# Attention with one PSUM bank for the products with V and three for the ring, the block's copy one unit sooner on ScalarE, and transposes ahead of products in a unit

## The chip, the cores and the metric

The kernel runs on one core of a Trainium2 chip. The metric is the time of one execution on the device in microseconds (us).

## What is computed

One block of a MetaFormer on 8 images of 512 channels by 32 x 32 positions (1024 tokens): a layer norm over channels, attention with 8 heads of 64 with its projections and residual, then a layer norm over tokens and a mixture of 16 experts, each of which takes the 128 tokens with the highest affinities of every image.

```python
def reference(x, Wq, bq, Wk, bk, Wv, bv, Wo, bo, gate_weight, w1, b1, w2, b2):
    x = x + attention(ln_c(x))         # 8 heads, softmax over 1024 keys
    t = to_tokens(x)
    t = t + experts(ln_t(t))           # gate, top 128 of each expert, gelu MLP, scatter-add
    return from_tokens(t)
```

The parameter names are shortened here (`L0_conv_Wq` and so on), and `attention` stands for q, k, v projections, softmax(q k / 8) v and the output projection.

## The kernel before

Every engine has its own program, written out by hand in `attention` as a function per engine; the order of the work is the order of the code, and engines meet by semaphores alone. Products run on single-precision operands split into a high part and a low part, so most results in PSUM are read twice: ScalarE writes the high part to SBUF, VectorE subtracts it and writes the low part.

An image's attention is 64 units (`UNITS`): 4 pairs of heads (`PAIRS`), 2 heads each, 8 slices of 128 queries. A unit s means, in this order over three engines:

- TensorE, `scores`: 4 matmuls into one of two places of `S` (L865).
- VectorE, `maximum` (L696); ScalarE, `exponentials` into `prob` (L494).
- TensorE, `turn_probs` (L876): 8 transposes of `prob`, in two sets of four (c = 0, 1), each set into one bank of `ring`.
- ScalarE, `high_of_probs` (L503), and VectorE, the low part (L754): each set from `ring` into `PT`, which holds two blocks.
- TensorE, `product_with_v` (L908): two units make a block m of 256 queries; a block takes 32 matmuls of V and `PT` into one of two banks `O[:, m % 2]`, in four parts of 4 matmuls of each high and low (part 0 and 1 in one unit, 2 and 3 in the next).
- ScalarE, `copy_output` (L552): the block from `O` into `oHL`; GpSimd adds its two halves and scales them.

TensorE in its loop step s does the scores of unit s, the transposes of unit s-2 and two parts of block (s-5)//2 (`turn_and_multiply`). ScalarE in its step s does the exponential of unit s-1, at even s a copy of block (s-8)//2, then `high_of_probs` of unit s-2. For an even unit u that one waits until block u//2-2 is finished, since it shares its half of `PT`:

```python
if u // 2 >= 2 and u % 2 == 0 and c == 0:
    act.wait_ge(pv_done, j * BLOCKS + u // 2 - 1)
```

At s = 16, 32 and 48 `project_pair` (L818) makes q and k of the next pair: 48 matmuls into the ring, 12 for each of 4 results. The step before it does no products; they come first in the step of the projection.

The 8 banks of PSUM are `S` (4), `ring` (2, used in turn by number k of the ring's step) and `O` (2). A step of the ring waits until VectorE has read the step two before it (`ring_lo`); part 0 of block m waits until block m-2 has been copied (`o_copied`). Between images, `O` takes the V projection (two banks in turn), the gate's logits and their transposes, and the ring the norm's transposes.

After all images, `experts` runs; nothing of it is touched.

Of the kernel before, what the change touches and what calls it, by code (L numbers as in the profile page):

```python
# [16 lines left out]
F32 = mybir.dt.float32  # L17
# [6 lines left out]
P = 128  # L24
# [29 lines left out]
def ring_probs(u, c):  # L54

    return NT + 4 * min(PAIRS, (u + 2) // UP + 1) + 2 * u + c

# [29 lines left out]
def attention(nc, x, wT, b_row, b_col, gate, out, n2_dram, aff_dram, ident):  # L87
# [8 lines left out]
    with ExitStack() as ctx:  # L96
# [61 lines left out]
        ring = ctx.enter_context(nc.psum_tensor("ring", [P, 2, 512], F32))  # L158
        O = ctx.enter_context(nc.psum_tensor("O", [P, 2, 512], F32))
# [303 lines left out]
        def _(act):  # L463
# [5 lines left out]
            def high_of_norm(j, i):  # L469
                k = ring_norm(i)  # L470
                act.wait_ge(ring_filled, j * RING + k + 1)
                nc.scalar.activation(nT[:, 0, :, i * P:(i + 1) * P],
                                     ring[:, k % 2, :].rearrange("p (k t) -> p k t", k=KC),
                                     ACT.Copy).then_inc(ring_hi, 1)
# [6 lines left out]
            def high_of_proj(j, p, r0=0, r1=4):  # L481
                for r in range(r0, r1):
                    k = ring_proj(p, r)
                    act.wait_ge(ring_filled, j * RING + k + 1)
                    cols = slice((r % 2) * 512, (r % 2) * 512 + 512)
                    for odd in range(2):
                        rows = slice(D * odd, D * odd + D)
                        dst = kd[rows, odd, 0, cols] if r < 2 else qs[rows, odd, cols]
                        nc.scalar.activation(dst, ring[rows, k % 2, :], ACT.Identity,
                                             bias=bqk[rows, 1 - r // 2, p:p + 1]).then_inc(ring_hi if odd else even_hi, 1)  # L490
# [6 lines left out]
            def high_of_probs(j, u):  # L497
                for c in range(2):
                    k = ring_probs(u, c)
                    act.wait_ge(ring_filled, j * RING + k + 1)  # L500
                    if u // 2 >= 2 and u % 2 == 0 and c == 0:
                        act.wait_ge(pv_done, j * BLOCKS + u // 2 - 1)
                    nc.scalar.activation(PT[:, 0, u // 2 % 2, 4 * c:4 * c + 4, u % 2 * P:u % 2 * P + P],  # L503
                                         ring[:, k % 2, :].rearrange("p (m q) -> p m q", m=4),
                                         ACT.Copy).then_inc(ring_hi, 1)
# [33 lines left out]
            def image(b, last):  # L539
# [5 lines left out]
                def copy_output(m):  # L545
                    act.wait_ge(pv_done, b * BLOCKS + m + 1)
                    if m >= BLOCKS - HEAD_BLOCKS:
                        cols = slice(m % HEAD_BLOCKS * QC, m % HEAD_BLOCKS * QC + QC)
                        nc.scalar.activation(Rs[D:2 * D, cols], O[D:2 * D, m % 2, QC:2 * QC], ACT.Copy)
# [37 lines left out]
                def copy_logits(h):  # L587
                    act.wait_ge(logits, b * 2 + h + 1)
                    nc.scalar.activation(affT[:, 512 * h:512 * h + 512], O[0:E, h, :], ACT.Copy
                                         ).then_inc(logits_copied, 1)  # L590
# [19 lines left out]
                for i in range(2):  # L610
                    act.wait_ge(affT_filled, b * 2 + i + 1)
                    nc.scalar.activation(affT[:, 512 * i:512 * i + 512], O[0:E, 1 - i, :], ACT.Copy
                                         ).then_inc(affT_copied, 1)
# [4 lines left out]
        def _(dve):  # L618
# [41 lines left out]
            def low_of_norm(j, i):  # L660
                k = ring_norm(i)
                dve.wait_ge(ring_hi, j * RING + k + 1)
                nc.vector.tensor_tensor(nT[:, 1, :, i * P:(i + 1) * P],
                                        ring[:, k % 2, :].rearrange("p (k t) -> p k t", k=KC),
                                        nT[:, 0, :, i * P:(i + 1) * P].bitcast(F32),
                                        ALU.subtract).then_inc(ring_lo, 1)

            def sum_of_v(j, i):

                dve.wait_ge(v_filled, j * NT + i + 1)  # L670
                if i >= 4:
                    dve.wait_ge(v_lo, j * NT + i - 3)
                nc.vector.tensor_tensor(tok[:, i % 4, :], O[:, i % 2, :], bv_bc[:, :], ALU.add).then_inc(v_sum, 1)

            def low_of_proj(j, p, beside=None):
                for r in range(4):
                    if beside is not None:
                        beside(r)
                    k = ring_proj(p, r)
                    cols = slice((r % 2) * 512, (r % 2) * 512 + 512)  # L680
                    for odd in range(2):
                        if odd:
                            dve.wait_ge(ring_hi, j * RING + k + 1)
                        else:
                            dve.wait_ge(even_hi, j * (4 * PAIRS) + 4 * p + r + 1)
# [3 lines left out]
                        last_lo = nc.vector.scalar_tensor_tensor(  # L689
                            out=lo, in0=ring[rows, k % 2, :], scalar=bqk[rows, 1 - r // 2, p:p + 1],  # L690
                            in1=hi.bitcast(F32), op0=ALU.add, op1=ALU.subtract)
                    last_lo.then_inc(ring_lo, 1)
# [31 lines left out]
            def image(b, last):  # L724
# [8 lines left out]
                for s in range(2, UNITS + 2):  # L733
# [16 lines left out]
                    for c in range(2):  # L750
# [4 lines left out]
                                                ring[:, k % 2, :].rearrange("p (m q) -> p m q", m=4),  # L755
# [42 lines left out]
                lgp = O[:, 0, 0:NT * E].rearrange("p (i e) -> p i e", e=E)  # L798
# [15 lines left out]
        def _(pe):  # L814
# [8 lines left out]
            def turn_norm(j, i, first):  # L823

                k = ring_norm(i)
                pe.wait_ge(norm_done[0], j * NT + i + 1)
                if not first or i >= 2:
                    pe.wait_ge(ring_lo, j * RING + k - 1)
                for c in range(KC):
                    last_t = nc.tensor.transpose(ring[:, k % 2, c * P:(c + 1) * P], xt[:, i, c * P:(c + 1) * P], ident)  # L830
                last_t.then_inc(ring_filled, 1)

            def project_v(j, i):
# [3 lines left out]
                products(O[:, i % 2, :], [(nT[:, l, c, i * P:(i + 1) * P], wv[:, w, c, :])  # L837
                                          for c in range(KC) for l, w in HL]).then_inc(v_filled, 1)

            def project_pair(j, p, r0=0, r1=4):  # L840
# [29 lines left out]
            def turn_probs(j, u, c):  # L870
# [3 lines left out]
                pe.wait_ge(ring_lo, j * RING + k - 1)  # L874
                for m in range(4):
                    last_t = nc.tensor.transpose(ring[:, k % 2, m * P:(m + 1) * P],  # L876
# [19 lines left out]
            def image(b, last):  # L896
                def product_with_v(m, part):

                    head = m // QB
                    if part == 0:  # L900
                        if m == 0:
                            pe.wait_ge(v_lo, b * NT + NT)
                        if m >= 2:
                            pe.wait_ge(o_copied, b * BLOCKS + m - 1)
                        pe.wait_ge(ring_lo, b * RING + ring_probs(2 * m + 1, 1) + 1)
                    for t in range(2 * part, 2 * part + 2):
                        for l in range(2):
                            last_mm = nc.tensor.matmul(  # L908
                                O[:, m % 2, 0:QC],
# [6 lines left out]
                def inverse_sums(m):  # L916
# [4 lines left out]
                    for j in range(2):  # L921
                        last_t = nc.tensor.transpose(O[:, m % 2, QC + j * P:QC + (j + 1) * P],
# [94 lines left out]
                for i in range(NT):  # L1017
                    pe.wait_ge(n2_copied, b * NT + i + 1)
                    last_mm = products(O[0:E, i // 4, i % 4 * P:i % 4 * P + P],
# [11 lines left out]
                for i in range(NT):  # L1031
                    last_t = nc.tensor.transpose(O[:, 0, i * E:(i + 1) * E], affT[:, i * P:(i + 1) * P],
# [7 lines left out]
                for h in range(2):  # L1040
                    for i in range(4):
                        last_t = nc.tensor.transpose(O[0:E, 1 - h, i * P:(i + 1) * P], aff[:, 4 * h + i, :], ident)
# [392 lines left out]
```

## Time and profile before

| | before |
|---|---|
| median of 3 runs | 3221.65 us (3219.97 to 3221.84) |
| profiled execution | 3216.83 us |
| its span, first to last instruction | 3215.0 us |
| mean granted TensorE clock | 0.984 |
| two units in the steady part of a head | 5.45 us |

In views by groups, a line of the kernel, its engine and operation are followed by busy time, mean duration and the idle time of the engine just before, with what ended it ("<-ACT PT L503": ScalarE's write at L503). In the order of time, a row has the start, the duration until the last of its instructions ended, and how many there are. PE is TensorE, PEld its loading of weights, ACT ScalarE, DVE VectorE, POOL GpSimd.

### The profile page before, as it was taken

The numbers are of one execution on the slowest core, as the hardware profiler recorded it, in microseconds if no ns is written. First come the engines' busy times: TensorE is split into PE (matmuls) and PEld (weight loads), VectorE is DVE, ScalarE is ACT, GpSimd is POOL, SyncE is SP. The second block draws the span as 40 slices with busy tenths as digits, with TensorE's granted clock in tenths as the row PEclk, the third lists the DMA queues.
The fourth block names the chain that finished last, engine by engine and source line by source line (L and its number), as shares of the span: only waits on it lengthen the run. The fifth ranks groups of instructions, "written<-read, shape, count | busy, mean of one in ns | idle before, by whom it ended". The sixth has DMA issues, their size and how long they took to land. (4 is left out here: it accounts for less than half of the span.)

```text
span 3215.0 us, 49747 instructions
## 1 busy us (share of the span) xinstructions
PE 3059.6 (95%) x18114; PEld 2627.4 (82%) x18114; DVE 2278.2 (71%) x3481; ACT 1850.1 (58%) x3353; POOL 1093.1 (34%) x1112
## 2 busy tenths in 40 slices
PE   6999999999999999999999999999917999999998
PEld 5988889888888888887988889888816788888886
DVE  5887688688768877876888688587775655655653
ACT  4876678477657857774876678477612333333332
POOL 1225224322512351252225124322513444444443
PEclk9999999999999999999999999999968999999999
DMA  7122121321321132113123121311224666666564
GB/s 236 37 60 106 64 63 50 112 67 37 105 88 50 50 115 77 37 57 118 58 60 109 61 63 57 105 41 37 63 96 94 135 141 133 135 143 137 129 144 59
DMA packets 121438, 283.59 MB, mean 88 GB/s; under 512 B 22417, under 2 KB 30609, under 8 KB 110481
## 3 DMA queue, kind: packets, MB, share of 16 engines
q1 hardware_dynamic: 92560, 213.72, 20.1%
q0 software_dynamic: 28672, 67.13, 11.8%
q8 instruction: 130, 2.13, 0.3%
q14 instruction: 76, 0.61, 0.1%
HBM read 173.08 MB, written 74.15 MB: 77 GB/s over the span
## 5 line engine op out<-in xcount | busy, mean ns | idle before, releaser
L754 DVE TENSOR_TENSOR PT<-ring,PT 128x512 fp32r<-128x512 f32 x1024 | 676.5, 686 | 160.4 <-ACT PT L503 142.2
L503 ACT ACTIVATE PT<-ring 128x512 fp32r<-128x512 f32 x1024 | 582.7, 597 | 169.8 <-PE ring L876 87.2
L908 PE MATMUL O<-PT,V 128*128 128x256 f32 x4096 | 673.0, 289 | 0.0
L696 DVE TENSOR_REDUCE nmax<-S 128x1 f32<-128x1024 f32 x512 | 619.8, 1211 | 71.7 <-PE S L865 71.7
L876 PE MATMUL ring<-ident,prob 128*128 128x128 f32 x4096 | 614.1, 273 | 15.3 <-DVE PT L754 12.9
L908 PEld LDWEIGHTS O<-PT,V 128*128 128x128 f32 x4096 | 575.4, 189 | 40.2
L865 PE MATMUL S<-kd,qs 128*128 128x512 f32 x2048 | 599.0, 414 | 2.7 <-ACT prob L494 1.7
L494 ACT ACTIVATE prob<-S,nmax 128x1024 f32<-128x1024 f32 x512 | 571.3, 1116 | 36.4 <-DVE nmax L696 36.4
L432 POOL COPY oS<-oHL 64x256 f32<-64x256 f32 x256 | 100.9, 394 | 1282.3 <-ACT oHL L552 1276.3
L876 PEld LDWEIGHTS ring<-ident,prob 128*128 128x128 f32 x4096 | 463.9, 139 | 55.3 <-issue 49.5
L865 PEld LDWEIGHTS S<-kd,qs 128*128 128x128 f32 x2048 | 347.2, 189 | 50.5 <-issue 6.0
L1389 PE MATMUL p<-ws,hT 128*128 128x512 f32 x1536 | 375.6, 397 | 0.7 <-DVE hT L1295 0.7
L1352 PE MATMUL p<-xT,ws 128*128 128x512 f32 x1536 | 355.0, 390 | 1.5 <-DVE xT L1280 1.5
L1352 PEld LDWEIGHTS p<-xT,ws 128*128 128x128 f32 x1536 | 289.4, 188 | 62.0 <-issue 1.9
L1389 PEld LDWEIGHTS p<-ws,hT 128*128 128x128 f32 x1536 | 281.2, 188 | 57.7 <-DVE hT L1295 1.9
L1189 POOL DMA_INDIRECT out_dram<-y,idxc x128 | 202.7, 1584 | 282.5 <-ACT y L1257 250.2
L818 PE MATMUL ring<-nT,wqk 128*128 128x512 f32 x1152 | 267.1, 391 | 3.7 <-DVE PT L754 3.7
L818 PEld LDWEIGHTS ring<-nT,wqk 128*128 128x128 f32 x1152 | 214.4, 188 | 51.0 <-issue 7.9
L1245 ACT ACTIVATE hf<-p,b1s 128x512 f32<-128x512 f32 x128 | 88.3, 690 | 233.0 <-PE p L1352 233.0
L434 POOL TENSOR_TENSOR oT<-oHL,oS 64x256 f32<-64x256 f32 x256 | 188.9, 738 | 20.5
L1232 ACT ACTIVATE xT<-xr 128x512 fp32r<-128x512 f32 x128 | 73.0, 598 | 211.0 <-PE xr L1362 211.0
L947 PE MATMUL S<-wo,nT 128*128 128x512 f32 x768 | 191.3, 398 | 0.0
(115 smaller groups left out, 3457.7 us busy)
## 6 DMA issues: line engine op xcount, KB each, us to landing
kd<-kd SPq DMA_DIRECT2D x128, 256.0 KB, 3.6
wraw<-w_dram SPq DMA_DIRECT2D x32, 1024.0 KB, 7.3
wqk<-wqk_split SPq DMA_DIRECT2D x24, 1024.0 KB, 4.8
xt<-x_dram SPq DMA_DIRECT2D x16, 1024.0 KB, 7.5
Rs<-rinv_rows SPq DMA_DIRECT2D x56, 256.0 KB, 3.4
PT<-wv_split SPq DMA_DIRECT2D x7, 2048.0 KB, 8.9
oT<-x_dram SPq DMA_DIRECT2D x24, 512.0 KB, 3.3
out_dram<-oT SPq DMA_DIRECT2D x48, 256.0 KB, 8.3
```

The costliest lines, as they stand in the source:

```text
L494: nc.scalar.activation(prob[:, s % 2, :], S[:, s % 2, :], ACT.Exp, bias=nmax[:, s:s + 1], accum_out=rsum[:, s:s + 1]).then_inc(exp_done, 1)
L503: nc.scalar.activation(PT[:, 0, u // 2 % 2, 4 * c:4 * c + 4, u % 2 * P:u % 2 * P + P], ring[:, k % 2, :].rearrange("p (m q) -> p m q", m=4 ...
L696: nc.vector.tensor_reduce(nmax[:, s:s + 1], S[:, s % 2, :], AX.X, ALU.max, negate=True).then_inc(max_done, 1)
L754: nc.vector.tensor_tensor(PT[:, 1, here[0], here[1], here[2]], ring[:, k % 2, :].rearrange("p (m q) -> p m q", m=4), PT[:, 0, here[0], her ...
L818: last_mm = nc.tensor.matmul(dst, l, r, start=(n == 0), stop=(n == len(pairs) - 1))
L865: last_mm = nc.tensor.matmul(S[:, s % 2, 512 * m:512 * m + 512], qs[:, odd, i * P:(i + 1) * P], kd[:, odd, l, 512 * m:512 * m + 512], star ...
L876: last_t = nc.tensor.transpose(ring[:, k % 2, m * P:(m + 1) * P], prob[:, u % 2, (4 * c + m) * P:(4 * c + m + 1) * P], ident)
L908: last_mm = nc.tensor.matmul(O[:, m % 2, 0:QC], V[:, t, head // 2, 2 * (head % 2):2 * (head % 2) + 2, :].rearrange("p h d -> p (h d)"), PT ...
L947: last_mm = nc.tensor.matmul(S4[:, i % 4, :], oS[:, l, c, i * P:(i + 1) * P], wo[:, w, c, :], start=(c + n == 0), stop=(c == KC - 1 and n ...
L1189: pool.indirect_dma_start(out=out_rows, out_offset=bass.IndirectOffsetOnAxis(ap=idxc[:, k, G * g + j:G * g + j + 1], axis=0), in_=y[:, g, ...
L1352: last = nc.tensor.matmul(dst, l, r, start=(n == 0), stop=(n == len(pairs) - 1))
L1389: prod = nc.tensor.matmul(p2[:, j, :], hT[:, l, c, j * P:(j + 1) * P], ws[:, k, w, KC + c, :], start=(c + n == 0), stop=(c == KC - 1 and n ...
```

## The change

`O` becomes one bank (`[P, 2 * QC]`), the ring gets three. From the first set of transposes of unit 3 on, each image's ring steps go round three banks, before that round two (`SLOT`, `LAST_USE`); each waits for the step that last used its bank. Everything outside the block loop that used two banks of `O` uses `wide(0)`, the bank `O`, and `wide(1)`, the ring's third. Part 0 of block m waits for the copy of block m-1. ScalarE copies block (s-7)//2 at odd s, and in a unit the transposes of set c come ahead of the products of part c.

```diff
+def ring_slots():
+
+    narrow = ring_probs(3, 0), RING
+    slots, used, last_use = [], {}, []
+    for k in range(2 * RING):
+        i = k % RING
+        slot = (i - narrow[0]) % 3 if narrow[0] <= i < narrow[1] else i % 2
+        slots.append(slot)
+        last_use.append(used.get(slot, k) - RING)
+        used[slot] = k
+    return slots[RING:], last_use[RING:]
+
+
+SLOT, LAST_USE = ring_slots()
...
-        ring = ctx.enter_context(nc.psum_tensor("ring", [P, 2, 512], F32))
-        O = ctx.enter_context(nc.psum_tensor("O", [P, 2, 512], F32))
+        ring = ctx.enter_context(nc.psum_tensor("ring", [P, 3, 512], F32))
+        O = ctx.enter_context(nc.psum_tensor("O", [P, 2 * QC], F32))
+
+        def wide(i):
+
+            return O[:, :] if i == 0 else ring[:, 2, :]
...
-                    nc.scalar.activation(oHL[:, m % 2, :], O[:, m % 2, 0:QC], ACT.Copy).then_inc(o_copied, 1)
+                    nc.scalar.activation(oHL[:, m % 2, :], O[:, 0:QC], ACT.Copy).then_inc(o_copied, 1)
...
-                    if s >= 8 and s % 2 == 0:
-                        copy_output((s - 8) // 2)
+                    if s >= 7 and s % 2 == 1:
+                        copy_output((s - 7) // 2)
                     high_of_probs(b, s - 2)
                     if s in EARLY_AT:
                         high_of_output(EARLY_AT.index(s))
+                copy_output(BLOCKS - 3)
                 high_of_probs(b, UNITS - 1)
                 high_of_output(EARLY)
-                copy_output(BLOCKS - 3)
+                copy_output(BLOCKS - 2)
                 if not last:
                     root(0, b + 1, slice(0, NT))
-                copy_output(BLOCKS - 2)
                 high_of_output(EARLY + 1)
...
                     k = ring_proj(p, r)
-                    pe.wait_ge(ring_lo, j * RING + k - 1)
-                    products(ring[:, k % 2, :],
+                    if j * RING + LAST_USE[k] >= 0:
+                        pe.wait_ge(ring_lo, j * RING + LAST_USE[k] + 1)
+                    products(ring[:, SLOT[k], :],
...
                 pe.wait_ge(exp_done, j * UNITS + u + 1)
-                pe.wait_ge(ring_lo, j * RING + k - 1)
+                if j * RING + LAST_USE[k] >= 0:
+                    pe.wait_ge(ring_lo, j * RING + LAST_USE[k] + 1)
...
-                        if m >= 2:
-                            pe.wait_ge(o_copied, b * BLOCKS + m - 1)
+                        if m >= 1:
+                            pe.wait_ge(o_copied, b * BLOCKS + m)
...
                     for c in range(2):
+                        turn_probs(b, u, c)
                         if m >= 0:
                             product_with_v(m, 2 * half + c)
-                        turn_probs(b, u, c)
```

How it moves ScalarE's work, in the first head of an image, here before. L494 is the exponential, L503 the split of a set of transposes (the one with `pv_done` waits for a block's last product), L552 the copy of a block:

```order
L494 ACTIVATE prob,rsum<-S,nmax 128x1024 [waits max_done,ring_filled]
L503 ACTIVATE PT<-ring 128x4x128 [waits ring_filled] x2
L494 ACTIVATE prob,rsum<-S,nmax 128x1024 [waits max_done,ring_filled]
L552 ACTIVATE oHL<-O 128x256 [waits o_sum,pv_done]
L503 ACTIVATE PT<-ring 128x4x128 [waits pv_done,ring_filled]
L503 ACTIVATE PT<-ring 128x4x128 [waits ring_filled]
L494 ACTIVATE prob,rsum<-S,nmax 128x1024 [waits max_done,ring_filled]
L503 ACTIVATE PT<-ring 128x4x128 [waits ring_filled] x2
```

And after the change, from the same exponential, where the lines are L515, L524 and L573:

```order
L515 ACTIVATE prob,rsum<-S,nmax 128x1024 [waits max_done,ring_filled]
L573 ACTIVATE oHL<-O 128x256 [waits o_sum,pv_done]
L524 ACTIVATE PT<-ring 128x4x128 [waits ring_filled] x2
L515 ACTIVATE prob,rsum<-S,nmax 128x1024 [waits max_done,ring_filled]
L524 ACTIVATE PT<-ring 128x4x128 [waits pv_done,ring_filled]
L524 ACTIVATE PT<-ring 128x4x128 [waits ring_filled]
L515 ACTIVATE prob,rsum<-S,nmax 128x1024 [waits max_done,ring_filled]
L573 ACTIVATE oHL<-O 128x256 [waits o_sum,pv_done]
```

The copy moved from behind the second exponential after a wait for `pv_done` to behind the first; two splits and an exponential stand between that wait and the copy of the block that it waited for.

TensorE's order where one block ends and the next begins, before. L865 are scores, L876 transposes, L908 products with V; the wait for `o_copied` is for block m-2:

```order
L908 MATMUL O<-PT,V 128x256 x4
L876 MATMUL ring<-ident,prob 128x128 [waits ring_lo,exp_done]
L876 MATMUL ring<-ident,prob 128x128 x3
L908 MATMUL O<-PT,V 128x256 x4
L876 MATMUL ring<-ident,prob 128x128 [waits ring_lo,exp_done]
L876 MATMUL ring<-ident,prob 128x128 x3
L865 MATMUL S<-kd,qs 128x512 [waits exp_done]
L865 MATMUL S<-kd,qs 128x512 x3
L908 MATMUL O<-PT,V 128x256 [waits ring_lo,o_copied]
L908 MATMUL O<-PT,V 128x256 x3
```

And after the change (L887, L899, L931), where the wait for `o_copied` is for block m-1:

```order
L931 MATMUL O<-PT,V 128x256 x4
L899 MATMUL ring<-ident,prob 128x128 [waits ring_lo,exp_done]
L899 MATMUL ring<-ident,prob 128x128 x3
L931 MATMUL O<-PT,V 128x256 x4
L887 MATMUL S<-kd,qs 128x512 [waits exp_done]
L887 MATMUL S<-kd,qs 128x512 x3
L899 MATMUL ring<-ident,prob 128x128 [waits ring_lo,exp_done]
L899 MATMUL ring<-ident,prob 128x128 x3
L931 MATMUL O<-PT,V 128x256 [waits ring_lo,o_copied]
L931 MATMUL O<-PT,V 128x256 x3
L899 MATMUL ring<-ident,prob 128x128 [waits ring_lo,exp_done]
L899 MATMUL ring<-ident,prob 128x128 x3
```

The last four products of a block now stand behind the second set of transposes and right ahead of the scores, and between them and the next block's first product there are the scores and one set of transposes.

## Rows read from the trace of the kernel before

**Rows 1.** The page, busy time of each engine with its share of the span.
```profile
PE 3059.6 (95%) x18114; PEld 2627.4 (82%) x18114; DVE 2278.2 (71%) x3481; ACT 1850.1 (58%) x3353; POOL 1093.1 (34%) x1112
```

**Rows 2.** Groups by line: busy us, mean ns of one | idle before.
```profile
L908 PE MATMUL O<-PT,V 128*128 128x256 f32 x4096 | 673.0, 289 | 0.0
...
L503 ACT ACTIVATE PT<-ring 128x512 fp32r<-128x512 f32 x1024 | 582.7, 597 | 169.8 <-PE ring L876 87.2 <-PE O L908 69.7 <-PE O L922 8.8
...
L552 ACT ACTIVATE oHL<-O 128x256 f32<-128x256 f32 x256 | 99.1, 387 | 1.0
```

**Rows 3.** Order of time, TensorE, 434 to 441 us: start, duration, instructions.
```profile
434.48 0.71 PE L908 MATMUL O<-PT,V 128*128 128x256 f32 x4
...
435.39 1.17 PE L865 MATMUL S<-kd,qs 128*128 128x512 f32 x4
...
436.39 0.62 PE L908 MATMUL O<-PT,V 128*128 128x256 f32 x4
...
436.85 0.60 PE L876 MATMUL ring<-ident,prob 128*128 128x128 f32 x4
...
437.21 0.71 PE L908 MATMUL O<-PT,V 128*128 128x256 f32 x4
...
437.76 0.60 PE L876 MATMUL ring<-ident,prob 128*128 128x128 f32 x4
...
440.84 0.47 PE L865 MATMUL S<-kd,qs 128*128 128x512 f32 x1
```

**Rows 4.** Order of time, ScalarE, 434 to 441 us.
```profile
435.29 1.09 ACT L503 ACTIVATE PT<-ring 128x512 fp32r<-128x512 f32 x2 [0.38 <-PE O L908]
...
436.26 1.12 ACT L494 ACTIVATE prob<-S,nmax 128x1024 f32<-128x1024 f32 x1
...
438.89 1.11 ACT L494 ACTIVATE prob<-S,nmax 128x1024 f32<-128x1024 f32 x1
...
439.98 0.39 ACT L552 ACTIVATE oHL<-O 128x256 f32<-128x256 f32 x1
```

**Rows 5.** Order of time around a projection: TensorE, then VectorE, then ScalarE.
```profile
394.98 0.71 PE L908 MATMUL O<-PT,V 128*128 128x256 f32 x4
...
398.24 1.19 PE L908 MATMUL O<-PT,V 128*128 128x256 f32 x8
...
399.59 11.12 PE L818 MATMUL ring<-nT,wqk 128*128 128x512 f32 x48 [0.15 <-DVE PT L754]
...
410.90 1.20 PE L908 MATMUL O<-PT,V 128*128 128x256 f32 x8
...
413.13 0.63 PE L876 MATMUL ring<-ident,prob 128*128 128x128 f32 x4
...
414.52 0.63 PE L908 MATMUL O<-PT,V 128*128 128x256 f32 x4
...
411.47 1.51 DVE L689 SCALAR_TENSOR_TENSOR qs<-ring,bqk,qs 64x512 fp32r<-64x512 f32 x2 [0.49 <-ACT qs L489]
...
413.07 0.69 DVE L754 TENSOR_TENSOR PT<-ring,PT 128x512 fp32r<-128x512 f32 x1
...
413.68 1.21 DVE L696 TENSOR_REDUCE nmax<-S 128x1 f32<-128x1024 f32 x1
...
414.99 1.12 ACT L494 ACTIVATE prob<-S,nmax 128x1024 f32<-128x1024 f32 x1 [0.60 <-DVE nmax L696]
```

**Rows 6.** Order of time, ScalarE, a copy of the output's high part.
```profile
543.65 0.63 ACT L543 ACTIVATE nT<-oT 128x512 fp32r<-128x512 f32 x1
544.17 1.12 ACT L494 ACTIVATE prob<-S,nmax 128x1024 f32<-128x1024 f32 x1
```

**Rows 7.** Stretches: length, busy (count) of PE, PEld, DVE, ACT, POOL; granted clock.
```profile
69.00:76.00 7.00, 4.70 (x19) 3.26 (x19) 4.08 (x5) 4.22 (x7) 0.00 (x0) 0.76 0.57 209
2546.00:2552.00 6.00, 4.42 (x22) 3.33 (x22) 4.39 (x7) 1.21 (x2) 4.78 (x5) 1.00 0.47 131
434.00:441.00 7.00, 7.00 (x56) 6.66 (x55) 6.31 (x9) 5.91 (x13) 1.53 (x4) 1.00 0.01 1
```

More of the change, by code:

```diff
@@ L472, in high_of_norm @@
                 nc.scalar.activation(nT[:, 0, :, i * P:(i + 1) * P],
-                                     ring[:, k % 2, :].rearrange("p (k t) -> p k t", k=KC),
+                                     ring[:, SLOT[k], :].rearrange("p (k t) -> p k t", k=KC),
                                      ACT.Copy).then_inc(ring_hi, 1)
@@ L488, in high_of_proj @@
                         dst = kd[rows, odd, 0, cols] if r < 2 else qs[rows, odd, cols]
-                        nc.scalar.activation(dst, ring[rows, k % 2, :], ACT.Identity,
+                        nc.scalar.activation(dst, ring[rows, SLOT[k], :], ACT.Identity,
                                              bias=bqk[rows, 1 - r // 2, p:p + 1]).then_inc(ring_hi if odd else even_hi, 1)
@@ L503, in high_of_probs @@
                     nc.scalar.activation(PT[:, 0, u // 2 % 2, 4 * c:4 * c + 4, u % 2 * P:u % 2 * P + P],
-                                         ring[:, k % 2, :].rearrange("p (m q) -> p m q", m=4),
+                                         ring[:, SLOT[k], :].rearrange("p (m q) -> p m q", m=4),
                                          ACT.Copy).then_inc(ring_hi, 1)
@@ L663, in low_of_norm @@
                 nc.vector.tensor_tensor(nT[:, 1, :, i * P:(i + 1) * P],
-                                        ring[:, k % 2, :].rearrange("p (k t) -> p k t", k=KC),
+                                        ring[:, SLOT[k], :].rearrange("p (k t) -> p k t", k=KC),
                                         nT[:, 0, :, i * P:(i + 1) * P].bitcast(F32),
@@ L672, in sum_of_v @@
                     dve.wait_ge(v_lo, j * NT + i - 3)
-                nc.vector.tensor_tensor(tok[:, i % 4, :], O[:, i % 2, :], bv_bc[:, :], ALU.add).then_inc(v_sum, 1)
+                nc.vector.tensor_tensor(tok[:, i % 4, :], wide(i % 2), bv_bc[:, :], ALU.add).then_inc(v_sum, 1)
             def low_of_proj(j, p, beside=None):
@@ L689, in low_of_proj @@
                         last_lo = nc.vector.scalar_tensor_tensor(
-                            out=lo, in0=ring[rows, k % 2, :], scalar=bqk[rows, 1 - r // 2, p:p + 1],
+                            out=lo, in0=ring[rows, SLOT[k], :], scalar=bqk[rows, 1 - r // 2, p:p + 1],
                             in1=hi.bitcast(F32), op0=ALU.add, op1=ALU.subtract)
@@ L754, in image @@
                         nc.vector.tensor_tensor(PT[:, 1, here[0], here[1], here[2]],
-                                                ring[:, k % 2, :].rearrange("p (m q) -> p m q", m=4),
+                                                ring[:, SLOT[k], :].rearrange("p (m q) -> p m q", m=4),
                                                 PT[:, 0, here[0], here[1], here[2]].bitcast(F32),
@@ L797, in image @@
                 dve.wait_ge(logits_turned, b + 1)
-                lgp = O[:, 0, 0:NT * E].rearrange("p (i e) -> p i e", e=E)
+                lgp = wide(0)[:, 0:NT * E].rearrange("p (i e) -> p i e", e=E)
                 nc.vector.tensor_reduce(gmax[:, :], lgp, AX.X, ALU.max).then_inc(soft, 1)
@@ L827, in turn_norm @@
                 if not first or i >= 2:
-                    pe.wait_ge(ring_lo, j * RING + k - 1)
+                    pe.wait_ge(ring_lo, j * RING + LAST_USE[k] + 1)
                 for c in range(KC):
-                    last_t = nc.tensor.transpose(ring[:, k % 2, c * P:(c + 1) * P], xt[:, i, c * P:(c + 1) * P], ident)
+                    last_t = nc.tensor.transpose(ring[:, SLOT[k], c * P:(c + 1) * P], xt[:, i, c * P:(c + 1) * P], ident)
                 last_t.then_inc(ring_filled, 1)
@@ L836, in project_v @@
                     pe.wait_ge(v_sum, j * NT + i - 1)
-                products(O[:, i % 2, :], [(nT[:, l, c, i * P:(i + 1) * P], wv[:, w, c, :])
+                products(wide(i % 2), [(nT[:, l, c, i * P:(i + 1) * P], wv[:, w, c, :])
                                           for c in range(KC) for l, w in HL]).then_inc(v_filled, 1)
@@ L873, in turn_probs @@
                 pe.wait_ge(exp_done, j * UNITS + u + 1)
-                pe.wait_ge(ring_lo, j * RING + k - 1)
+                if j * RING + LAST_USE[k] >= 0:
+                    pe.wait_ge(ring_lo, j * RING + LAST_USE[k] + 1)
                 for m in range(4):
-                    last_t = nc.tensor.transpose(ring[:, k % 2, m * P:(m + 1) * P],
+                    last_t = nc.tensor.transpose(ring[:, SLOT[k], m * P:(m + 1) * P],
                                                  prob[:, u % 2, (4 * c + m) * P:(4 * c + m + 1) * P], ident)
@@ L908, in product_with_v @@
                             last_mm = nc.tensor.matmul(
-                                O[:, m % 2, 0:QC],
+                                O[:, 0:QC],
                                 V[:, t, head // 2, 2 * (head % 2):2 * (head % 2) + 2, :].rearrange("p h d -> p (h d)"),
@@ L1018, in image @@
                     pe.wait_ge(n2_copied, b * NT + i + 1)
-                    last_mm = products(O[0:E, i // 4, i % 4 * P:i % 4 * P + P],
+                    last_mm = products(wide(i // 4)[0:E, i % 4 * P:i % 4 * P + P],
                                        [(gate_sb[:, c, :], n2T[:, i % 2, c, :]) for c in range(KC)])
```

12 lines of the change are left out of this document (6 added, 6 removed).

## The prediction

> **What bounds the kernel now.** I read the page's busy times first, then the groups by line, then the order of time in two units of the attention loop, TensorE and ScalarE apart. The page says TensorE [rows 1], and the groups say where: the products with V have no idle time before them in 4096 instructions, while the split of the turned probabilities on ScalarE waits 169.8 us in all [rows 2]. A busy TensorE can be a modelled one, so the stretch itself has to be looked at.
>
> In the steady part of a head, two units of 8 scores, 16 transposes and 16 products repeat from 435.39 to 440.84 [rows 3], 5.45 us, with every group following the one before at once. TensorE is the bound there, at 2.73 us a unit. A unit now runs in the order scores (1.00 us to the next group's start), four products (0.46), transposes (0.36), four products (0.55), transposes.
>
> ScalarE is nearly as full, and one of its waits matters. The last product of a block starts its group at 434.48 and ends 0.71 later, at 435.19; ScalarE's split of the next even unit starts at 435.29 [rows 3, 4]. That split (`high_of_probs`, even unit, first half) waits for `pv_done`, because the block's half of `PT` must have been read. So ScalarE stands still until a block is finished, and what it does afterwards is a chain with a fixed length: two splits (435.29 to 436.26, 0.97 us), an exponential (438.89 to 439.98, 1.09), and only then, in the new order, the copy of the block (0.39) [rows 4, 2].
>
> **The change, part by part.** *The copy one unit sooner.* Before, the copy of block m stood behind two exponentials, but the next block had the other bank and did not wait for it. Now it stands behind one exponential, and the first product of block m+1 waits for it (`o_copied` of block m instead of m-1). Sooner in ScalarE's order is still after the two splits that wait for the block's own last product. From the end of that product: 0.10 until the split starts (435.19 to 435.29), 0.97, 1.09, 0.39, and from the end of the copy to TensorE. The last has no row of its own between these two engines. Below it lies 0; the nearest rows are VectorE releasing TensorE's transposes (411.47 + 1.51 = 412.98 to 413.13), 0.15 [rows 5], and I take that; twice it is the upper end. The sum is 2.70 us.
>
> *What covers it.* Between the last product of block m and the first of m+1 TensorE now has the scores of one unit and one set of four transposes: 1.00 + 0.36 = 1.36 us by the starts of their groups [rows 3]. The product's end (0.71 after its group's start) lies 0.16 behind the start of the group after it (0.55), so 1.20 us count against the 2.70. The rest, 1.50 us, is a wait in which TensorE does nothing: its matmuls go in order, and the second set of transposes stands behind the waiting product. Products after transposes take 0.55, after scores 0.46 [rows 3]; I read the 0.09 as weights that were not there yet, and expect the same after the wait: **1.59 us a block**, 7.04 instead of 5.45. Its ends: 1.26 (the release and the weights cost 0, and scores ahead of transposes take 0.09 more, which lengthens the cover) and 1.84 (release and start of the split twice as long).
>
> The Trainium skill, Perfetto Trace Analysis, Matmuls, says that independent groups of matmuls should rotate through PSUM banks so that the evacuation of one overlaps the next group. By that alone only the evacuation would be exposed: 0.10 + 0.39 + 0.15 = 0.64 us from the rows, under the cover of 1.20, and the sum would be 0. The rows make it 1.59, since what stands in front of the copy counts, not the copy.
>
> *Where this holds.* An image has 32 blocks, 31 hand-overs. In 23 of them the pattern is the ordinary one (units 7 to 13 of the first head pair, six in each of the next two, seven in the last): 23 x 1.59 = 36.6 us. Three of these have a copy of the output's high part between the splits and the exponential, 0.52 us more each (543.65 to 544.17) [rows 6]: 1.6. The last of them has a second copy out of the bank, 0.39: 0.4.
>
> Before each of the three later projections the block is put off behind a second set of transposes. There TensorE already takes 3.26 us from the block's last product to the next block's first (394.98 to 398.24) [rows 5]; the chain asks for 0.71 + 2.70 + 0.09 = 3.50, so 0.2 each: 0.7.
>
> After each projection the block's end is at 410.90 + 1.20 = 412.10. VectorE ends the projection's low parts at 412.98, then does one low part (0.61 to the next start) and the maximum (1.21), the exponential starts 0.09 after that (414.90 to 414.99) [rows 5]. Without the old copy in front the first low part is ready when VectorE is, so the exponential starts at 414.89, the copy ends 1.48 later at 416.37, and the product can start at 416.52 instead of 414.52: 2.00 us. The first product of the projection loses its 0.15 wait, since it waits one ring step further back: 1.85 each, 5.5.
>
> The last two hand-overs lie beside nine products with wo each, about 2 us by 0.23 of the projection (11.12 us for 48) [rows 5], and have no exponential in their chain: 0.97 + 0.39 + 0.39 + 0.25 = 2.0. Nothing.
>
> *The third ring bank and the new order of transposes.* They remove waits that hardly exist (0.15 at 24 projections, counted above) and add no instruction. VectorE's low part of a set of transposes now has to be done three sets later instead of two. Each group takes what it took; order alone moves no time in a TensorE that has no wait. I cost both at nothing.
>
> *The rest.* Other uses of the two banks (the V projection, the gate's logits, their transposes) take the same two places in the same order with the same waits. Norms, the first head pair's projection and the experts are not touched. 0.
>
> Sum per image: 36.6 + 1.6 + 0.4 + 0.7 + 5.5 = 44.8; for 8 images 358 us. The profiled execution took 3216.83, so 3575 by its own clock. The median of the runs shown lies 4.8 above it (0.15%), which I leave within the rounding: **3577 us**.
>
> **The rivals.**
> *The bank is free in time; not slower.* The price of the single bank is set by one point: if the chain is under the cover of 1.20 us, no product waits. It would be, if ScalarE had done the two splits and the exponential before the block ended, leaving 0.64. Then only the 24 waits of 0.15 go: 3213 to 3217 in the profiled execution's time, no change, or faster by a little. Against it: the split does wait for the block's end in the rows (idle until 435.29), and the copy is behind it in order. 5 in 100.
>
> *The clock falls.* A TensorE that stops for over a microsecond in every block could be given the lower level, 1.2 GHz. In 69 to 76 us, among long waits, the granted clock was 0.76; in 2546 to 2552, with 4.42 us busy of 6.00, it stayed at 1.00; in the steady part it is 1.00 [rows 7]. The forecast has TensorE working in most of the 7.04 us, more like the second. At 0.76, TensorE's part of a block, 7.04 - 2.70 = 4.34 us, would take 5.71, 1.4 us more in some 230 blocks: 320 us more, 3900. A rule of the Trainium skill (TensorE: Matmul & The Clock Gate, A second HAM failure mode: psum-queue depth-cycling) points that way: a kernel that cycled PSUM banks idled briefly between groups, and its clock went back and forth between both levels. By that rule this rival; the stretch at 2546 speaks against it. 6 in 100.
>
> *A second wait per block.* If a set of transposes after the stop has to wait for VectorE's low part, it costs about the time of such a set, 0.36, in 8 x 23 blocks: 66 us more, 3643. Against it: ScalarE works 2 x (0.97 + 1.09) + 0.39 = 4.5 of the 7.04 us, so that VectorE gets its inputs early. 4 in 100.
>
> **How the numbers follow.** 85 in 100 for the forecast, whose own ends are 23 x 1.26 and 23 x 1.84 in an image (7.6 us below, 5.7 above, 61 and 46 in all): 3516 to 3623. The range takes a little more on both sides for the hand-overs at the projections, which have only one row each to go by: 3500 to 3630. It leaves out all three rivals. A measurement of this kernel tells about 0.2% (6.4 us) from no change. Faster 0.02, within it 0.03, slower 0.95.
>
> **What would show it.** In the changed profile: idle time of TensorE before the first product of a block, released by ScalarE's copy, some 1.2 to 1.4 us as seen from a modelled end, some 200 times; two units in 7.0 us instead of 5.45; ScalarE's wait for the product's end grown from 0.38 to over 1 us; a granted clock of 1.00 in the loop; the wrap between images and the experts as they were. Wrong would be: steady units at 2.73 us (the first rival), a clock under 0.95 (the second), or a wait on VectorE before transposes (the third).

## The result, and the profile after

The changed kernel took 3567.82 us (median of 4 runs, 3565.46 to 3569.13), the kernel before beside it 3220.81 (3217.56 to 3221.84). The ratio is 1.108, 95% interval 1.107 to 1.109: slower by 347 us, where 355 (3577 against the median of 3221.65 shown before) had been forecast. The profiled execution took 3569.13 us, 352 more than the profiled one before, against 358 in the sum of terms.

The page of the changed kernel, busy time of each engine and its share of the span, answers to [rows 1]:

```profile
span 3567.3 us, 49754 instructions
...
PE 3117.0 (87%) x18114; PEld 2627.2 (74%) x18114; DVE 2308.8 (65%) x3481; ACT 1835.2 (51%) x3353; POOL 1091.7 (31%) x1112
```

No engine got more work: ScalarE and VectorE did the same in a longer time, and TensorE, which was busy for 95% of its span, now is for 87%. Its groups by line (busy us, mean ns | idle before, releasers) say where it stands, with [rows 2] to compare:

```profile
L931 PE MATMUL O<-PT,V 128*128 128x256 f32 x4096 | 724.7, 302 | 298.7 <-ACT oHL L573 298.7
...
L524 ACT ACTIVATE PT<-ring 128x512 fp32r<-128x512 f32 x1024 | 588.4, 602 | 528.2 <-PE O L931 311.6 <-PE ring L899 193.4 <-PE O L945 21.8
...
L573 ACT ACTIVATE oHL<-O 128x256 f32<-128x256 f32 x256 | 100.1, 391 | 0.4
```

The products with V, which had no idle time before them, have 298.7 us, all of it ended by the copy of a block. And the splits on ScalarE wait 311.6 us for products with V, where it was 69.7. Each of the two engines waits for the other: a loop.

Its parts are in the order of time on TensorE, in the steady part of a head, as [rows 3] were (start, duration, instructions, idle before):

```profile
470.31 1.09 PE L887 MATMUL S<-kd,qs 128*128 128x512 f32 x4
...
472.51 0.72 PE L931 MATMUL O<-PT,V 128*128 128x256 f32 x4
473.06 1.08 PE L887 MATMUL S<-kd,qs 128*128 128x512 f32 x4
473.99 0.60 PE L899 MATMUL ring<-ident,prob 128*128 128x128 f32 x4
475.83 0.74 PE L931 MATMUL O<-PT,V 128*128 128x256 f32 x4 [1.25 <-ACT oHL L573]
476.41 0.60 PE L899 MATMUL ring<-ident,prob 128*128 128x128 f32 x4
...
482.85 0.74 PE L931 MATMUL O<-PT,V 128*128 128x256 f32 x4 [1.25 <-ACT oHL L573]
```

and on ScalarE, as [rows 4]:

```profile
473.32 1.09 ACT L524 ACTIVATE PT<-ring 128x512 fp32r<-128x512 f32 x2 [1.59 <-PE O L931]
474.30 1.12 ACT L515 ACTIVATE prob<-S,nmax 128x1024 f32<-128x1024 f32 x1
475.29 0.21 ACT L515 ACTIVATION_READ_ACCUMULATOR prob<-S,nmax 128x1 f32 x1
475.39 0.39 ACT L573 ACTIVATE oHL<-O 128x256 f32<-128x256 f32 x1
```

Read them as one chain. A block's last products end at 472.51 + 0.72 = 473.23. The split starts at 473.32, the exponential at 474.30, the copy at 475.39, which ends at 475.78; the next block's product starts at 475.83. From one block's first product to the next one's it is 482.85 - 475.83 = 7.02 us, where it was 5.45.

Around a projection, TensorE again, to compare with [rows 5]:

```profile
443.94 0.74 PE L931 MATMUL O<-PT,V 128*128 128x256 f32 x4 [1.24 <-ACT oHL L573]
...
449.92 0.63 PE L899 MATMUL ring<-ident,prob 128*128 128x128 f32 x4 [0.20 <-DVE PT L775]
450.95 1.21 PE L931 MATMUL O<-PT,V 128*128 128x256 f32 x8 [0.41 <-ACT oHL L573]
452.00 11.07 PE L839 MATMUL ring<-nT,wqk 128*128 128x512 f32 x48
...
468.83 0.73 PE L931 MATMUL O<-PT,V 128*128 128x256 f32 x4 [1.53 <-ACT oHL L573]
```

The block ahead of the projection comes 450.95 - 443.94 = 7.01 us after the one before it, and the block behind it 17.88 us later; before, those 17.88 were 414.52 - 398.24 = 16.28. The second projection of every image but the last takes 536.93 - 518.17 = 18.76, since VectorE does the next image's norm there (L655) before it takes up the low part:

```profile
518.17 1.22 PE L931 MATMUL O<-PT,V 128*128 128x256 f32 x8 [0.41 <-ACT oHL L573]
...
532.61 0.64 DVE L655 BATCH_NORM_AGGREGATE mv<-stats 128x2 f32<-128x6 f32 x8
...
536.93 1.22 PE L931 MATMUL O<-PT,V 128*128 128x256 f32 x4 [2.37 <-ACT oHL L573]
```

### The profile page after: what moved, and what is told of

Its sections match the earlier page's. It is cut to its first block and busy times, and to the rows that moved or that the text cites. A ratio compares the mean times of both kernels' runs of the same rounds, so it can differ in the third digit from the quotient of the medians.

```text
span 3567.3 us, 49754 instructions
## 1 busy us (share of the span) xinstructions
PE 3117.0 (87%) x18114; PEld 2627.2 (74%) x18114; DVE 2308.8 (65%) x3481; ACT 1835.2 (51%) x3353; POOL 1091.7 (31%) x1112
## 5 line engine op out<-in xcount | busy, mean ns | idle before, releaser
L931 PE MATMUL O<-PT,V 128*128 128x256 f32 x4096 | 724.7, 302 | 298.7 <-ACT oHL L573 298.7
L524 ACT ACTIVATE PT<-ring 128x512 fp32r<-128x512 f32 x1024 | 588.4, 602 | 528.2 <-PE O L931 311.6
L931 PEld LDWEIGHTS O<-PT,V 128*128 128x128 f32 x4096 | 549.2, 190 | 355.3 <-ACT oHL L573 353.9
L899 PE MATMUL ring<-ident,prob 128*128 128x128 f32 x4096 | 616.6, 273 | 10.7 <-DVE PT L775 7.8
L515 ACT ACTIVATE prob<-S,nmax 128x1024 f32<-128x1024 f32 x512 | 571.1, 1115 | 38.3 <-DVE nmax L717 34.7
L887 PE MATMUL S<-kd,qs 128*128 128x512 f32 x2048 | 567.1, 399 | 1.9 <-ACT prob L515 1.7
L899 PEld LDWEIGHTS ring<-ident,prob 128*128 128x128 f32 x4096 | 488.9, 141 | 94.1 <-issue 25.0
L887 PEld LDWEIGHTS S<-kd,qs 128*128 128x128 f32 x2048 | 350.3, 189 | 52.0 <-issue 4.7
```

The source lines that it names most:

```text
L515: nc.scalar.activation(prob[:, s % 2, :], S[:, s % 2, :], ACT.Exp, bias=nmax[:, s:s + 1], accum_out=rsum[:, s:s + 1]).then_inc(exp_done, 1)
L887: last_mm = nc.tensor.matmul(S[:, s % 2, 512 * m:512 * m + 512], qs[:, odd, i * P:(i + 1) * P], kd[:, odd, l, 512 * m:512 * m + 512], star ...
L899: last_t = nc.tensor.transpose(ring[:, SLOT[k], m * P:(m + 1) * P], prob[:, u % 2, (4 * c + m) * P:(4 * c + m + 1) * P], ident)
L931: last_mm = nc.tensor.matmul(O[:, 0:QC], V[:, t, head // 2, 2 * (head % 2):2 * (head % 2) + 2, :].rearrange("p h d -> p (h d)"), PT[:, l, ...
```

## The experiments

The theory under test: the loss is the chain on ScalarE, that is, what stands between a block's end and its copy in ScalarE's order. The rivals: one bank as such, which a copy and products cannot share; and the new order of transposes, or VectorE's low parts behind the ring.

**The copy ahead of the splits.** An edit of the changed kernel:

```diff
-                    if s >= 7 and s % 2 == 1:
-                        copy_output((s - 7) // 2)
+                    if s >= 6 and s % 2 == 0:
+                        copy_output((s - 6) // 2)
                     high_of_probs(b, s - 2)
...
-                copy_output(BLOCKS - 3)
                 high_of_probs(b, UNITS - 1)
```

> The changed kernel, with ScalarE's copy of a block moved ahead of the two splits that also wait for the block's last product; bank, ring and the order of transposes as changed. Theory of the chain (what stands ahead of the copy sets the wait): from the block's end 0.10 + 0.39 + 0.15 = 0.64 us, less than the 1.1 to 1.2 us of scores and transposes, so the first product of the next block does not wait. What is late next is the exponential, 0.26 later than it would be: block's end to split and exponential and scores and block's end is 0.10 + 0.26 + 0.97 + 1.20 + 0.15 + 2.91 = 5.59 us against 5.45, 0.15 a block or a little more. 3255 us, 3235 to 3285. Rival (one bank as such costs the time, because copy and products cannot share it): 0.64 us a block stays, 3360. Rival (the new order of transposes or the ring's third bank does it): 3568 as before.

Measured: 3259.09 us (3258.37 to 3261.24), ratio 1.012 (1.011 to 1.014). Of the 347 us, 309 are gone by moving one instruction of 0.39 us past two splits and an exponential. There is still one bank. Its products wait for no copy any more:

```profile
L930 PE MATMUL O<-PT,V 128*128 128x256 f32 x4096 | 715.2, 299 | 0.0
...
L898 PE MATMUL ring<-ident,prob 128*128 128x128 f32 x4096 | 620.2, 274 | 21.5 <-DVE PT L774 18.0 <-ACT prob L515 3.1
```

Both rivals fall, the bank's 3360 and the order's 3568. The size was right, the place of what is left was not. I had put it on the exponential; but the second group shows that transposes wait for VectorE's low part. In the order of time of TensorE:

```profile
389.28 0.71 PE L930 MATMUL O<-PT,V 128*128 128x256 f32 x4
389.95 0.63 PE L898 MATMUL ring<-ident,prob 128*128 128x128 f32 x4
390.33 0.72 PE L930 MATMUL O<-PT,V 128*128 128x256 f32 x4
...
394.92 0.71 PE L930 MATMUL O<-PT,V 128*128 128x256 f32 x4
```

A block takes 394.92 - 389.28 = 5.64 us. The second set of transposes starts 0.67 after the first products (389.28 to 389.95), where 0.56 is usual with transposes first. VectorE's row says why; of its two instructions, the low part of the first split ends at 389.80:

```profile
389.11 1.29 DVE L774 TENSOR_TENSOR PT<-ring,PT 128x512 fp32r<-128x512 f32 x2 [0.90 <-ACT PT L524]
```

It is late since the split had to let the copy go first, and its end frees the ring bank that these transposes need; they start 0.15 later. Of the 0.19 us over 5.45, some 0.05 is the order with transposes first (two units of 2.75 us in the changed kernel make 5.50), the rest this wait.

**The copy between the splits and the exponential.** The same edit, with the copy one line lower:

```diff
                     high_of_probs(b, s - 2)
+                    if s >= 6 and s % 2 == 0:
+                        copy_output((s - 6) // 2)
```

> The changed kernel, with the copy behind the two splits but ahead of the exponential. Theory of the chain: the 1.09 us of the exponential leave the chain, the block's loop goes from 7.01 to 5.92 us, 0.47 over 5.45. With 184 ordinary hand-overs 86 us, and some 12 at the projections: 3318 us, 3290 to 3345. Rival (the bank as such): the same as with the copy ahead of the splits. Rival (order or ring): 3568.

Measured: 3300.01 us (3298.43 to 3303.18), ratio 1.025 (1.023 to 1.027). The same bank and the same copy at a third place take a third time, which settles it between chain and bank:

```profile
394.25 0.74 PE L930 MATMUL O<-PT,V 128*128 128x256 f32 x4 [0.16 <-ACT oHL L573]
...
400.16 0.74 PE L930 MATMUL O<-PT,V 128*128 128x256 f32 x4 [0.16 <-ACT oHL L573]
```

The block's loop is 400.16 - 394.25 = 5.91 us, where 7.01 less an exponential of 1.09 makes 5.92. The total came 18 us under my figure: I had added half a microsecond at each of 24 projections on top of the ordinary blocks. In the trace the stretches ahead of and across a projection are 0.45 and 0.16 us shorter than before the change (see the last experiments), and the block behind it, which counts as an ordinary one, is 0.5 longer.

**Only the order inside a unit undone.**

```diff
                     for c in range(2):
-                        turn_probs(b, u, c)
                         if m >= 0:
                             product_with_v(m, 2 * half + c)
+                        turn_probs(b, u, c)
```

> The changed kernel, with only the order inside a unit undone: products ahead of transposes again. Theory of the chain: between a block's last product and the next block's first lie one set of transposes and the scores of a unit, as before in another order, and the chain on ScalarE is the same, so 7.01 us a block stay: 3568 us, 3550 to 3585. Rival (transposes ahead of products cause the loss): back to 3221.

Measured: 3594.76 us (3591.07 to 3596.68), ratio 1.116 (1.114 to 1.118). Not a microsecond comes back, so the order of transposes does not make the loss of the changed kernel. But it is 27 us slower than the changed kernel, and my range ended at 3585. The ordinary block is what was expected, 485.71 - 478.72 = 6.99 us:

```profile
478.72 0.74 PE L931 MATMUL O<-PT,V 128*128 128x256 f32 x4 [1.25 <-ACT oHL L573]
...
485.71 0.75 PE L931 MATMUL O<-PT,V 128*128 128x256 f32 x4 [1.25 <-ACT oHL L573]
```

What differs is the clock, by the view of the core (span, mean granted clock): 0.975 here, 0.983 in the changed kernel. A stretch of this trace where it fell (length, busy of PE, PEld, DVE, ACT, POOL, granted clock), and an ordinary one after it:

```profile
1140.00:1144.00 4.00, 4.00 (x19) 3.86 (x20) 0.74 (x2) 1.21 (x3) 1.12 (x2) 0.57 0.00 0
1147.00:1155.00 8.00, 6.04 (x42) 5.06 (x40) 5.95 (x9) 5.76 (x12) 1.12 (x2) 1.00 0.11 33
```

The trace has 19 blocks of 8.3 to 9.1 us instead of 7.0 or 7.5, the changed kernel's has 5 of 8.3 to 8.6. The same fall shows in four hand-overs from block 29 to 30 (7.76 us for 6.15). Eighteen more of them than in the changed kernel, at 1.6 us, are 29 us. At the end of each image the hand-overs from block 28 to 29 and from 30 to 31 take 0.4 and 0.5 us more, 7 in all, and ordinary blocks and the stretches between images are shorter by about as much.

**The copy one unit sooner, with two banks.** The kernel before, with the change's edits of ScalarE's loop and of the end of an image, and nothing else.

> The kernel before, with only ScalarE's copy one unit sooner; two banks for the products, two for the ring, the old order. Theory of the chain: the next block has the other bank and waits for the copy of the block before, which is long done, so 3221 us, 3212 to 3230. Rival (the copy at its new place delays ScalarE's splits, whoever waits for the bank): some of the 347 us, 3300 or more.

Measured: 3228.62 us (3228.39 to 3231.69), ratio 1.003 (1.002 to 1.004). With a second bank the same chain costs nothing in an ordinary block, which stays at 5.45 us. The 8 us that are there come from elsewhere: by the starts of blocks in both traces, the hand-over from block 29 to 30 grew from 6.8 to 7.35 us, 0.55 in each image, about half of it all; most of the rest is in the blocks with a copy of the output's high part (5.54 for 5.45 us) and across the projections (16.34 for 16.28). ScalarE's order at the end of an image was changed too, and there the copy of block 29 now stands ahead of the last unit's splits. No run takes that by itself, so it is the likely cause of the longer hand-over and not a shown one.

**The ring's third bank left idle.** The changed kernel with `slot = i % 2` in `ring_slots`.

> The changed kernel with the ring's third bank left idle: the ring goes round two banks everywhere, all else as changed. Theory of the chain: the first transposes after a block's end then wait for VectorE's low part of the first split, which starts with the block's end: 0.10 + 0.60 + 0.10 + 0.69 + 0.15, some 1.6 us after the end, and they take 0.35, so they are done at 2.0, before the copy lets the product go at 2.7. They fit into the wait: 3568 us, 3555 to 3590. Rival (VectorE's low parts, not the copy, hold TensorE, and the third bank softens it): slower than the changed kernel by up to 0.9 us a block, 3700 or more.

Measured: 3582.2 us (3580.51 to 3583.22), ratio 1.112 (1.111 to 1.114). Within the range of the chain's theory, and 14 us over the changed kernel. Ordinary blocks are the same, 7.02 us. Most of the difference, 24 times 0.3 to 0.36 us, sits at the projections: from the block ahead to the one behind, 470.30 - 452.06 = 18.24 us where it was 17.88.

```profile
452.06 1.21 PE L931 MATMUL O<-PT,V 128*128 128x256 f32 x8
453.36 11.18 PE L839 MATMUL ring<-nT,wqk 128*128 128x512 f32 x48
...
470.30 0.74 PE L931 MATMUL O<-PT,V 128*128 128x256 f32 x4 [1.34 <-ACT oHL L573]
```

So in the changed kernel the third bank does something, and the loop hides most of it. Taking the loop away should let it show.

**Copy ahead of the splits, products ahead of transposes.** The first and the third edit together.

> One bank for the products and three for the ring, with ScalarE's copy ahead of the splits (as in the first experiment) and products ahead of transposes in a unit (as before the change). Theory of the chain: the copy is hidden, and with products first a block ends 0.4 us sooner in its unit, so that the loop by the exponential and the scores takes 0.10 + 0.26 + 0.97 + 1.20 + 0.15 + 2.53 = 5.21 us, under TensorE's 5.45: no wait in ordinary blocks. In the three blocks of an image with a copy of the output's high part 0.52 comes in: 5.73, 0.28 too much, 7 us in all; the 0.15 wait ahead of 24 projections goes, 3.6 us. 3224 us, 3216 to 3232. Rival (a single bank costs something whatever the order): more than the 3259 of the first experiment less 8, so 3245 or more.

Measured: 3204.61 us (3203.04 to 3206.5), ratio 0.995 (0.994 to 0.996): faster than the kernel before by 16 us, and out of my range on the good side; what I had left out shows in the next run. Against the first experiment 54 us are gone by the order of transposes alone. In the changed kernel the same order made no gain, since the wait for the copy stood over it.

**The same, with the high parts of the output at odd steps.**

```diff
-EARLY_AT = [50, 52, 54, 55, 57, 59]
+EARLY_AT = [49, 51, 53, 55, 57, 59]
```

> As the one before, and the copies of the output's high parts at odd steps of ScalarE (49, 51, 53, 55, 57, 59), out of the loop by the exponential. Theory of the chain: the 7 us in those blocks go, the 3.6 us at the projections stay as a gain: 3217 us, 3209 to 3224, the same as the kernel before or a little faster. Rival (single bank costs): as above, 3245 or more.

Measured: 3200.91 us (3200.3 to 3204.11), ratio 0.994 (0.993 to 0.996): 19 us faster than the kernel before. The two intervals overlap, so that the last step's gain is shown by the traces alone: the three blocks with a high part take 5.63 to 5.72 us without it and 5.45 with it. No product waits for the single bank here:

```profile
L930 PE MATMUL O<-PT,V 128*128 128x256 f32 x4096 | 673.8, 289 | 0.0
```

The gain over the kernel before is around the projections, in TensorE's order of time:

```profile
394.88 1.22 PE L898 MATMUL ring<-ident,prob 128*128 128x128 f32 x8
395.85 1.19 PE L930 MATMUL O<-PT,V 128*128 128x256 f32 x8
396.88 11.07 PE L838 MATMUL ring<-nT,wqk 128*128 128x512 f32 x48
...
411.62 0.64 PE L930 MATMUL O<-PT,V 128*128 128x256 f32 x4
```

From the first products ahead of the projection to those behind it, 411.62 - 395.85 = 15.77 us against 16.28 in [rows 5]; and the block ahead of it, 6.42 us in this trace, took 6.80 before. Together 0.9 us, 24 times, 21 us.

**The last one with the ring's third bank left idle.**

> The last one (one bank for the products, copy ahead of the splits, products first, high parts at odd steps) with the ring's third bank left idle. It was some 19 us faster than the kernel before, and its stretches around a projection are 0.38 and 0.5 us shorter each, 24 times, 21 us in all. Theory A (the third ring bank takes away VectorE's waits around a projection): with two banks they come back, 3221 us, 3214 to 3228. Theory B (the copy at its new place, which no longer stands between a projection's last high part and the next split, makes the gain): 3201 us, 3196 to 3207.

Measured: 3262.39 us (3259.36 to 3262.84), ratio 1.013 (1.011 to 1.015). Theory B is out, and A is right in its direction and far too small: the third bank is worth 61 us, not 20. The waits around a projection are back (the block ahead of it 7.19 us, the stretch behind 16.3). What I had left out are the ordinary blocks:

```profile
433.15 0.62 PE L930 MATMUL O<-PT,V 128*128 128x256 f32 x4
433.73 0.63 PE L898 MATMUL ring<-ident,prob 128*128 128x128 f32 x4
434.12 0.72 PE L930 MATMUL O<-PT,V 128*128 128x256 f32 x4
...
438.80 0.62 PE L930 MATMUL O<-PT,V 128*128 128x256 f32 x4
```

A block takes 438.80 - 433.15 = 5.65 us; the transposes start 0.58 behind the products ahead of them, where [rows 3] had 0.46. The copy ahead of the splits delays VectorE's low part, and with a ring of two the next transposes need that bank. In VectorE's row the first of the two ends at 433.59:

```profile
432.90 1.29 DVE L774 TENSOR_TENSOR PT<-ring,PT 128x512 fp32r<-128x512 f32 x2 [0.78 <-ACT PT L524]
```

About 0.18 us in 144 ordinary blocks are 26 us, 1.3 us at 24 projections 31, and 0.9 us at each image's hand-over from block 29 to 30 another 7; the blocks behind a projection give back 4. So the third bank pays for the early copy, and the early copy pays for the single bank, which in turn gives the ring its third.

## Why the prediction was right

It was right in its sign and mechanism, and in its size partly by luck. The images' own blocks took 341 us more, 7.5 of them by the clock (below), where the sum had 358. Another 11 us lie where the sum had nothing: 5.6 between images, 2.5 ahead of the first block and 3.1 behind the last one; the last two differ by as much between other traces here. So the 352 for 358 is closer than the terms are. Point by point:

- *A wait per block, made of a chain and its cover.* The chain was put at 2.70 us and is 473.23 to 475.83, 2.60. The piece that I had taken from VectorE's release, 0.15, is 0.05 from ScalarE (475.78 to 475.83). The cover was put at 1.20 and is 1.11 (473.23 to 473.99 + 0.35). The two errors almost cancel, which is luck: a wait of 1.49 for 1.50.
- *0.09 for weights after the wait.* The products after the wait take 0.58 to the next group (475.83 to 476.41), after transposes without a wait 0.55 to 0.56, so 0.02 to 0.03 is all that the wait adds. The rest is in the unit: with transposes first it takes 473.06 - 470.31 = 2.75 us, where two units took 5.45. "Order alone moves no time" was off by 0.02 a unit. Block by block 7.02 was measured, 7.04 forecast.
- *The special places.* Ahead of a projection, 7.01 for 6.80, 0.2 as forecast. Behind it 1.60 us more (17.88 against 16.28), forecast 1.85: the projection starts 1.05 behind the first products (450.95 to 452.00) where it was 1.35 (398.24 to 399.59), 0.30 sooner and not 0.15, and the release is 0.05 and not 0.15. That is so at 17 of the 24 projections; the second one of every image but the last takes 18.76 (518.17 to 536.93 above), for the norm on VectorE. The kernel before had the same norm at the same place, and its delay showed one block later, in a hand-over of 6.41 us that the sum had counted as an ordinary one of 5.45. Both stretches together grew by 3.1 us at every projection, where 1.85 and 1.59, 3.44, had been forecast: some 8 us too much in all. The three blocks with a high part took 7.51 us, 0.50 over an ordinary one, forecast 0.52; the one with a second copy 7.75 for 5.71, 2.04, forecast 1.98.
- *Nothing at the last two hand-overs.* They came out shorter, by 0.8 and 0.4 us, 10 in all, and the seven stretches between images longer, by 0.6 to 1.1: terms that the sum left out, and whose cause no run tells.
- *The rule on rotating banks.* The Trainium skill (Perfetto Trace Analysis, Matmuls) has independent groups of matmuls rotate through PSUM banks, so that the evacuation of one overlaps the matmuls of the next. If the evacuation were all that a single bank exposes, as the prediction read it, 0.64 us would lie under the cover and nothing be lost. The changed kernel does not bear that out, and the versions with the copy right behind the block's end do: 0.39 us of copy out of the only bank, and no product waits for it.
- *The clock's rival, 6 in 100.* It did happen, but in 5 of 248 hand-overs and not in all, as an addition of about 8 us. Its price, 1.4 us a block, was near: these were 1.4 to 1.6 longer.
- *The first rival, the bank free in time.* Its point of decision was the right one. It is not met by the changed kernel, and the experiments met it by moving the copy alone.
- *The third ring bank and the order costed at next to nothing.* That held in the changed kernel within some 14 us (the ring of two) and was wrong as a view of the idea. With the copy out of the way the order is worth 54 us and the third bank 61; I counted the 0.15 us of idle time that the profile shows ahead of a projection, and the stretches ahead of and across it had 0.9 us to give.

## What to carry to other kernels

A buffer that is read once and short can be single, if the instruction that empties it stands right behind the event that fills it in the order of its engine; whatever stands between the two, and is more than the writer's other work covers, is paid by the writer in every round. So count the chain from the fill to the release, in the reader's order, against the work that the writer has in between. And when a change with a good idea loses, try its parts at other places before it is dropped: here the same banks, with one instruction moved and one order undone, went from 11% slower to 0.5% faster.

## What was not expected of the hardware

The granted clock fell inside the loop. The changed kernel's trace on TensorE, in a row of blocks with longer waits (1.77 us, where a high part is in the chain) and then the first ordinary one:

```profile
285.19 0.75 PE L931 MATMUL O<-PT,V 128*128 128x256 f32 x4 [1.77 <-ACT oHL L573]
...
292.70 0.74 PE L931 MATMUL O<-PT,V 128*128 128x256 f32 x4 [1.77 <-ACT oHL L573]
...
294.19 1.87 PE L887 MATMUL S<-kd,qs 128*128 128x512 f32 x4
295.86 1.05 PE L899 MATMUL ring<-ident,prob 128*128 128x128 f32 x4
...
301.29 0.74 PE L931 MATMUL O<-PT,V 128*128 128x256 f32 x4 [1.24 <-ACT oHL L573]
```

and the stretch:

```profile
294.00:297.50 3.50, 3.50 (x15) 3.00 (x15) 1.92 (x2) 2.13 (x4) 2.53 (x3) 0.53 0.00 0
```

At 294 us the level went to the lower one, 1.2 GHz, and scores and transposes took almost twice their time (1.87 for 1.09, 1.05 for 0.60); at 301 all is as before, 8.59 us after the block's start instead of 7.01. The other images' same blocks, with the same wait of 1.77 us, kept the upper level. The other four falls stand behind the second projection of images two to five, after the loop's longest stop, 2.37 to 2.43 us (the row at 536.93 above); images one, six and seven have that stop and no fall. So it is not decided by the wait alone.

Between the blocks of an image, three of the ten traces show such falls: 5 in the changed kernel, 5 with the ring's third bank idle, 23 with products first, which loses the most by it. These are the three with one bank and the exponential ahead of the copy, and so with a stop in every block; the other seven show none. The rule of the Trainium skill (TensorE: Matmul & The Clock Gate, A second HAM failure mode: psum-queue depth-cycling) that frequent short idling between groups of matmuls can move the clock back and forth agrees with that, in a small way; what decides which block it hits, no run shows.
